# Attention with routed feed-forward on one core: value products in groups of four slots, one row-sum group per head pair

## The reference

```python
latent_bll = jnp.einsum('bld,dc->blc', x_bld, Wkv_down)
attn = jnp.einsum('bqhd,bkhd->bhqk', q_blhd, k_blhd) / jnp.sqrt(jnp.asarray(HD, dtype=x_bld.dtype))
attn = jax.nn.softmax(jnp.where(mask, attn, neg_inf), axis=-1)
y_blhd = jnp.einsum('bhqk,bkhd->bqhd', attn, v_blhd)
...
x = _layernorm(x + _L0_attn_ref(x, ...), axis=-1)
x = _layernorm(x + _L0_ffn_ref(x, ...), axis=-1)
```

## Time and profile before

| what | us |
|---|---|
| median of 3 runs (lowest, highest) | 2690.92 (2690.39, 2691.18) |
| the profiled execution | 2683.09 |
| its span | 2681.3 |
| TensorE busy | 2494.3 (93%) |
| GpSimd busy | 1701.7 (63%) |
| VectorE busy | 1550.2 (58%) |
| ScalarE busy | 1002.2 (37%) |
| attention pairs, from the first scores of pair 0 | from 51.4 to about 2320 |

### The profile page before, as it was taken

The page is one execution under the profiler, slowest core; times in us unless marked ns, Lnnn a source line. Parts: engine busy times, 40 slices in busy tenths (PEclk is TensorE's granted clock), DMA queues, the critical chain, the costliest instruction groups (busy, mean ns, idle before and its releaser), DMA issues.

```text
span 2681.3 us, 35897 instructions
## 1 busy us (share of the span) xinstructions
PE 2494.3 (93%) x12072; PEld 1588.2 (59%) x12072; DVE 1550.2 (58%) x4378; ACT 1002.2 (37%) x1496; POOL 1701.7 (63%) x1671
## 2 busy tenths in 40 slices
PE   6999999999999999999999999999999999869996
PEld 4555665556655665566556655566556655646663
DVE  4566556665666566655665566656665665235553
ACT  3344334442444334433444244424443344112222
POOL 1677656865687658766786568656876578414444
PEclk7999999999999999999999999999999999879998
DMA  2121100200020001100110002000200011135441
GB/s 81 56 80 56 37 13 13 68 17 13 17 63 18 13 13 41 43 13 17 27 53 17 9 17 67 17 13 17 60 21 13 13 40 43 44 105 161 153 155 57
DMA packets 97062, 118.91 MB, mean 44 GB/s; under 512 B 12480, under 2 KB 75976, under 8 KB 96880
## 3 DMA queue, kind: packets, MB, share of 16 engines
q1 hardware_dynamic: 89712, 99.98, 13.3%
q0 software_dynamic: 7168, 16.64, 1.7%
HBM read 46.91 MB, written 37.90 MB: 32 GB/s over the span
## 4 chain that ended last, share of the span: by engine, by line
PE 63%; POOL 17%; issue 11%; DVE 5%; ACT 2%; DMA 0%; POOLq 0%; SPq 0%; ACTq 0%; DVEq 0%
PE value_ps L683 14%; POOL sums L464 10%; PE turned_ps L660 8%; PE row_ps L636 7%; PE turned_ps L663 7%; PE misc_ps L584 6%; PE turned_ps L844 5%; PE misc_ps L702 4%; PE misc_ps L693 4%; POOL probs L440 2%; PE value_ps L857 2%; PE misc_ps L857 2%; ACT probs L904 1%; POOL slots_x L497 1%; DVE masked_row L1056 1%
## 5 line engine op out<-in xcount | busy, mean ns | idle before, releaser
L904 ACT ACTIVATE probs<-turned_ps 128x1024 f32<-128x1024 f32 (+3 forms) x768 | 616.8, 811 | 959.6 <-PE turned_ps L663 951.3
L464 POOL TENSOR_TENSOR sums<-sums,probs 128x1024 f32<-128x1024 f32 (+3 forms) x512 | 830.2, 1622 | 23.2 <-ACT probs L904 14.2
L1056 DVE CUSTOM_DVE_ANT_0 masked_row<-row_ps,future 128x384 bf16<-128x384 f32 (+3 forms) x1024 | 464.2, 488 | 407.4 <-PE row_ps L636 406.2
L683 PE MATMUL value_ps<-probs,lat_keys 128*64 128x512 f32 (+3 forms) x3072 | 607.2, 507 | 44.7 <-POOL probs L440 41.3
L660 PE MATMUL turned_ps<-q_hl,lat_hi 128*128 128x512 f32 (+3 forms) x1536 | 569.6, 379 | 1.5 <-ACT fold_v L950 1.5
L663 PE MATMUL turned_ps<-q_max,lat_lo 65*128 65x512 f32 (+3 forms) x1536 | 528.0, 352 | 2.6 <-DMA q_max<-max_rows 2.6
L440 POOL TENSOR_SCALAR_AFFINE_SELECT probs<-probs 128x256 f32<-128x256 f32 x512 | 209.9, 410 | 498.1 <-ACT probs L904 497.4
L636 PE MATMUL row_ps<-lat_hi,q_hl 128*128 128x512 f32 (+3 forms) x1536 | 451.2, 365 | 14.2 <-DVE unit_max L1056 7.6
L460 POOL TENSOR_TENSOR sums<-probs 128x768 f32<-128x768 f32 (+1 forms) x128 | 268.6, 2098 | 229.9 <-ACT probs L904 229.9
L660 PEld LDWEIGHTS turned_ps<-q_hl,lat_hi 128*128 128x128 f32 x1536 | 293.8, 191 | 196.2 <-issue 148.3
L683 PEld LDWEIGHTS value_ps<-probs,lat_keys 128*64 128x64 f32 x3072 | 180.8, 137 | 348.8 <-issue 219.6
(11 more groups left out here) (183 smaller groups left out, 2408.7 us busy)
## 6 DMA issues: line engine op xcount, KB each, us to landing
q_max<-q_hl SPq DMA_DIRECT2D x256, 128.0 KB
slots_x<-zero_rows SPq DMA_DIRECT2D x8, 1290.0 KB, 6.2
ex_x<-slots_x SPq DMA_DIRECT2D x64, 129.0 KB, 3.5
x_in<-in_L_attn_x_bld SPq DMA_DIRECT2D x8, 1024.0 KB, 6.4
layer_out<-x_in SPq DMA_DIRECT2D x8, 1024.0 KB, 4.8
ex_w<-in_L_ffn_w_gate SPq DMA_DIRECT2D x32, 256.0 KB, 2.8
ex_w<-in_L_ffn_w_up SPq DMA_DIRECT2D x32, 256.0 KB, 3.2
ex_w<-in_L_ffn_w_down SPq DMA_DIRECT2D x32, 256.0 KB, 3.8
```

The costliest lines, as they stand in the source:

```text
L464: nc.gpsimd.tensor_tensor(sums[c][:, :, q0:BANK], sums[c][:, :, q0:BANK], now[:, :, q0:BANK], ALU.add).then_inc(added, 1)
L683: mm = nc.tensor.matmul(value_ps[h * LD:(h + 1) * LD, q0:BANK], lat_keys[b % 2][:, j, :], probs[:, n % NPROBS, h, q0:BANK], start=(j == 0) ...
L904: nc.scalar.activation(probs[:, n % NPROBS, :, q0:BANK], turned_ps[n % 2][:, :, q0:BANK], ACT.Exp).then_inc(exp_done, 1)
L1056: nc.vector.tensor_tensor_reduce(masked_row[n % 2][:, 0:width], row_ps[n % 2][:, 0:width], future[:, BANK - width:], scale=-1.0, scalar=-M ...
```

## The change

- `values` works on four slots at once (`VALUES = 4`), in slots 0, 4 and 8 instead of every second slot. `probs` has eight buffers instead of six.
- The units are spread as `COUNT = [4, 2, 1, 0, 4, 2, 2, 2, 4, 2, 1, 0]` instead of two in each slot. The first two of a slot stand ahead of the value products, the rest behind.
- Row sums are multiplied once per pair, for both halves: four products of 32 columns into the four quarters of misc_ps, in slot 4 of the next pair. The inversion (`invert_rows`) does both halves at once: two reciprocals, four copies of 32 x 16 elements that bring the quarters together, two transposes. `divide` moves from slots 0 and 6 to slots 6 and 10. There are three buffers `half_sums`.
- In slots with 256 or 128 queries both heads fit one bank, and the scores are two products instead of four.
- There is one `x_in` instead of two. It is loaded at p = 1 of the first batch, then at p = 5; the residual x is read once more from memory, into x1 itself, at p = 7.
- Side work changes slots: projections to 9, 10, 11 of p = 0 and 3, 5, 7, 9, 11 of p = 1; x1T to 3, 5, 7, 10 and the router to 11 of p = 2; `pos` to 7 of p = 3; `roots`, `variance`, `normalise` and the gate's exponentials with them. In the last pair the eight projections go to slots 8 to 11.

```diff
+    COUNT = [4, 2, 1, 0, 4, 2, 2, 2, 4, 2, 1, 0]
...
-    NPROBS = 6
+    NPROBS = 8
+    VALUES = 4
...
-                EARLY[gp, 4] = [("maxT", gp + 1, 0)]
+                EARLY[gp, 6] = [("maxT", gp + 1, 0)]
             if gp:
-                late[4].append(("sums", gp - 1, 1))
-            late[6].append(("sums", gp, 0))
+                late[4].append(("sums", gp - 1))
...
             if b and p == 0:
-                for i, t in enumerate((3, 5, 7, 10, 11)):
+                for i, t in enumerate((9, 10, 11)):
                     late[t].append(("proj", b - 1, i))
             if b and p == 1:
-                for i, t in enumerate((3, 5, 7)):
-                    late[t].append(("proj", b - 1, 5 + i))
...
+                for i, t in enumerate((3, 5, 7, 9, 11)):
+                    late[t].append(("proj", b - 1, 3 + i))
...
-                    if gp and t == 0:
-                        divide(gp - 1, 0)
-                    if gp and t == 6:
-                        divide(gp - 1, 1)
-                    if b and (p, t) in ((1, 0), (2, 0)):
+                    if gp and t in (6, 7 if gp == PAIRS - 1 else 10):
+                        divide(gp - 1, t // 7)
+                    if b and (p, t) in ((1, 8), (2, 2)):
                         roots(b - 1, p - 1)
...
+                if in_one_bank(t):
+                    nc.tensor.matmul(scores_of(n), lat_hi[b % 2][:, keys], q_hl[gp % 2][:, :, cols], start=True, stop=False)
+                    nc.tensor.matmul(scores_of(n), lat_lo[b % 2][:, keys], q_max[:, c, :, q0:BANK], start=False, stop=True
+                                     ).then_inc(turned_full, 1)
+                    return
...
                 for h in range(2):
-                    mm = nc.tensor.matmul(bank[h * LD:(h + 1) * LD, :], ones_f[:, :], sums[c][:, h, :], start=True, stop=True)
+                    for c in range(2):
+                        k = 2 * h + c
+                        mm = nc.tensor.matmul(bank[k * 32:(k + 1) * 32, :], ones_f[:, :], sums_of(gp, c)[:, h, :],
+                                              start=True, stop=True)
...
-                    for unit in UNITS_AT.get((gp, t), []):
+                    units = UNITS_AT.get((gp, t), [])
+                    for unit in units[:2]:
                         row_scores(*unit)
-                    if t % 2 == 0 and gp + t:
-                        values(gp * NSLOT + t - 2)
+                    if t % VALUES == 0 and gp + t:
+                        values(gp * NSLOT + t - VALUES)
+                    for unit in units[2:]:
+                        row_scores(*unit)
...
+            def invert_rows(gp):
+                wait_emptied(dve, ("sums", gp))
+                cols = sums_cols[:, :].rearrange("p (n q) -> p n q", q=32)[:, :, 0]
+                for c in range(2):
+                    nc.vector.reciprocal(rinv[:, c, :], cols).then_inc(inverse_done, 1)
+                dve.wait_ge(inverse_done, 6 * gp + 2)
+                for c in range(2):
+                    for h in range(2):
+                        src, dst = (64 * h + 32 * k for k in (c, 1 - c))
+                        nc.vector.tensor_copy(rinv[dst:dst + 32, c, :], rinv[src:src + 32, c, :]).then_inc(inverse_done, 1)
+                for c in range(2):
+                    dve.wait_ge(inverse_done, 6 * gp + 4 + 2 * c)
...
+                    nc.vector.transpose(rinv_rows[c][:, :], rinv[:, c, :].unsqueeze(2).to_broadcast([P, BANK // 32, 32])
+                                        ).then_inc(inverse_rows, 1)
```

More of the change, by code:

```diff
@@ L141, in build_layer @@
         send_idx = sb("send_idx", [P, NT], I32, attn)
-        x_in = [sb(f"x_in{i}", [P, NT, D], F32, attn) for i in range(2)]
+        x_in = sb("x_in", [P, NT, D], F32, attn)
         room = headsT[:, :, :].rearrange("p t d -> p (t d)")
@@ L463, in add_probs @@
                     pool.wait_ge(added, gp * NADD + ADDS_OF[t] - 1)
[L464 to L465 removed]
+                    total = sums_of(gp, c)[:, :, q0:BANK]
+                    nc.gpsimd.tensor_tensor(total, total, now[:, :, q0:BANK], ALU.add).then_inc(added, 1)
             def divide(gp, c):
@@ L666, in values @@
             def values(n0):
-                for n in (n0, n0 + 1):
+                for n in range(n0, n0 + VALUES):
                     gp, t = divmod(n, NSLOT)
```

134 lines of the change are left out of this document (68 added, 66 removed).

## The result

| | us |
|---|---|
| changed kernel, median of 4 runs (lowest, highest) | 3158.45 (3157.14, 3159.55) |
| kernel before, measured beside it, 4 runs | 2690.65 (2688.76, 2691.18) |
| ratio, 95% interval | 1.174 (1.172 to 1.176) |
| span of the profiled execution, before and after | 2681.3, 3155.4 |

The direction of the forecast was right and its size wrong: 2852 us were forecast, with 2910 as the upper end, and the kernel took 3158. The span grew by 474 us where the sum had 161.

The account below looks back on a forecast made before the run. TensorE, 93% busy, bounds the kernel; 2.06 us per plain pair is removed, but uncovered waits make it 3.1 longer. Plain pairs 102, p = 0 and 1 26, p = 2 and 6 28, end 5: +161, 2852 us (2700 to 2910).

Parts of the forecast that it names:

- the sum: Whole kernel: growth of plain pairs, side pairs and the end added up, +161 us on the profiled execution's 2683.1.
- side pairs: Pairs with projections, routing or latents: p = 0 -3.5 us, p = 1 +7.2, p = 2 and 6 +2 each, with misc_ps waits.
- What the value groups covered: Plain pair in six segments: waits formerly under value groups now show, 32.65 us against 29.55, 3.1 us longer.
- Segments 1 to 4: Plain pair, from query projection of slot 8 to scores of slot 5: 10.2, 1.9, 3.45 and 5.45 us.
- the division ahead of the mask: Segment 1, GpSimd: the second half's division moves ahead of the mask of slot 11 and adds 1.2 us.
- the wait on exponential 2: Segment 3, before the scores of slot 4: TensorE waits 1.1 us for the bank that exponential 2 reads.
- Segment 5, the small copies: Scores of slot 5 to value group of slot 8: 7.55 us, wait 2.0, VectorE's four small copies taken as 0.4.
- +2, between 0 and 4: Pairs p = 2 and p = 6: growth in us per pair, extra work partly covering segment 1's wait, partly waiting for misc_ps.
- Sums four at a time: Row sums, once per pair: four 32-column products run together in 0.86 us, saving 0.86 us per pair.
- the rival of 2907 us: Row sums: the four products don't run together, 0.86 x 64 = 55 us more than the forecast; chance 0.08.
- One-bank scores: Slots 3 and 11: two products of 256 columns replace four 128-wide ones, 2 x 0.25 = 0.50 us saved per pair.
- x_in, single buffer: Loads of 1 MB land in 6.4 us, ahead of their readers: no cost; if late, up to 6 us each, eight times.

Follow-up runs that it names:

- the kernel with groups of two: Changed kernel with both divisions moved (slot 6 ahead of the add, slot 8), then value groups of two slots and two units per slot: 2720.04 us.
- the run with fillers: Changed kernel plus 14 products with unused results in slot 7 of p = 3, 4, 5, 7 and every pair of batch 0: 3160.29 us.
- the two-slot kernel: Changed kernel with two-slot value groups, two units per slot, divisions in slots 6 (ahead of the add) and 8, `maxT` in slot 4, projections out of slot 9: 2647.59 us.
- the kernel of 3005 us: Changed kernel with the first half's division ahead of the add in slot 6 and the second half's moved from slot 10 to 8: 3005.11 us.

## Why the prediction was wrong in size

The sum missed 313 us. Three steps of it failed: the price of the small copies (98 to 103 us come back without the hold), the clock, which had no price at all (at most some 222 us, and it overlaps with the others), and the side pairs, whose waits for misc_ps had no segments (72 us come back with other slots, in the kernel with groups of two). How the rest is divided is open.

- **What the value groups covered**: right, and the core of the result. Groups of four slots, with the units spread to suit, cost 281 and 285 us in two pairs of runs. Segments 1 to 4 were met within 0.1 us, among them the division ahead of the mask and the wait on exponential 2.
- **Segment 5, the small copies**: wrong term. "I take 0.4" for four copies came from rows of 0.17 us in the earlier trace rows. They took 2.81 us. The rows were real, but GpSimd was idle when they ran (its add ended at 1021.34, and they stand at 1021.56 and 1021.63), while in the new place an add starts just ahead of the copies. The last sentence of the prediction named these copies as the weak point; the range gave them 0.3 to 0.7, which it should not have, since nothing beside them had been looked at. Taking the add away gives back 98 us, reciprocals instead 103. The trace of the kernel before already had a held small operation: VectorE's L1128, on four elements, takes 0.17 us in most places and 2.03 in seven of 16. Its timeline, and then that of GpSimd at the same time:

```profile
964.19 2.03 DVE L1128 TENSOR_SCALAR var_eps<-mean_var 128x4 f32<-128x4 f32 x1
```

```profile
963.82 2.38 POOL L464 TENSOR_TENSOR sums<-sums,probs 128x1024 f32<-128x1024 f32 x1
```

- **The clock**: a step that was missing. The forecast priced every product at the full clock although it forecast idle stretches of 2 us in each pair. From the end of the wait in slot 7 on (229.9 to 236.7) the clock is at its half level; 2.4 us per plain pair by the run with fillers. How much of the total it is was not isolated. An upper bound can be estimated: with the levels 1 and 0.5 alone, mean clocks of 0.906 and 0.972 are some 593 and 150 us at the half level, and 443 us more of it can hold no more than 222 us of lost TensorE time.
- **Side pairs**: mis-sized most. By class, from the first exponential of each pair, growth against forecast in us: 33 plain pairs 192 against 102; p = 0 and 1 118 against 26; p = 2 and 6, seven of each, 151 against 28; the last two pairs and what follows 15 against 5. p = 0, forecast 3.5 us shorter, grew by some 5.5: in batch 3 TensorE waits 9.7 us in it, 3.7 of them for the unit maxima as in a plain pair, and the clock is 0.90. For p = 6 "+2, between 0 and 4" was a guess, with no segment worked out. It grew by 13.2 us. Its waits in batch 3 grew from 3.2 to 13.2 us, and TensorE's busy time by 3.3, with fewer products, at a clock of 0.90. The longest waits:

```profile
PE misc_ps L662 <- DVE xT_lo L1045: 4.4, 1, 4.4
PE misc_ps L601 <- DVE q_hl L1069: 2.5, 1, 2.5
PE misc_ps L611 <- DVE q_hl L1069: 2.0, 1, 2.0
PE misc_ps L601 <- DVE lat_lo L1054: 1.8, 1, 1.8
PE value_ps L704 <- POOL probs L459: 1.8, 1, 1.8
```

  The first is the `maxT` that moved from slot 4 to slot 6: it needs misc_ps, which a transpose of x still holds until VectorE has finished the inversion, and in that the copies are held again (2.78 us). The forecast had followed every engine but not the one bank. Setting the slots back, with groups of two, took p = 6 from 39.5 to 36.5 us.
- **Sums four at a time**: right. The group of four 32-column products takes 223.28 - 222.29 = 0.99 us with the way out, where two of 64 took 0.96, and the four start within 0.02 us of each other; the rival of 2907 us fell.
- **One-bank scores**: over-sized. They gave 0.2 us per pair in the kernel before, where 0.5 was forecast.
- **x_in, single buffer**: no wait for x stands in any pair, as forecast; the only one, 7.7 us, is for the first load, before the pairs.

## What to carry to other kernels

Groups of work that look like overhead on the busiest engine may be the cover for its suppliers: before merging them, write down what each one hides, and give every shared bank a row of its own in that list, beside the engines. The price of an operation is read from a row only together with what the neighbouring engine does at that moment; in these kernels small VectorE copies and two-input operations beside long GpSimd adds cost the rest of the add, and one of them ahead of a critical result was worth replacing (here by reciprocals) or moving. A group whose durations have a median of 0.17 and a highest of 2.2 us is the sign; its mean hides it. A forecast with idle stretches on TensorE needs a second price, for what follows them at the lower clock.

## What the runs showed of the hardware that I had not expected

- A VectorE copy, a maximum with two inputs, and operations on eight elements in `pos` begin beside a running GpSimd add and end with it: 2.2 us instead of 0.17. The profile counts the time as the instruction's own and names no releaser, so it looks like a slow operation. Reciprocals and stream transposes beside the same adds keep their times (245 ns; 1.30 us for two). So does a subtraction with one input in PSUM and one in SBUF (L1069): 0.69 us beside adds and away from them.
- After waits of 3.67 us and of 1.62 us in an otherwise busy pair the products run at the half level (1.2 GHz) for several microseconds. Waits of 0.3 and 1.0 us in the two-slot kernel were not followed by that (clock 1.00 over its plain pairs), but neither was one of 1.74 us in the changed kernel, and in the kernel of 3005 us a low stretch follows no wait over 0.4 us.
- Four products of 32 columns side by side cost about what two of 64 do: 0.99 us for a group with the way out, against 0.96.
